# A new order of steps in the first block and in the recurrent block's sixteen slots

## Chip, cores, metric

One core of one Trainium2 chip. The time is device microseconds of one execution, the median of several runs.

## What is computed

Four blocks in a row over `x` (32 x 128 tokens x 512) with the context `ctx` of the same shape, all in float32. Cut to what matters here:

```python
# block 0: attention on the context, 32 query heads and 8 key heads of 16, a mask that is added, then layer norm
q, k, v = x @ Wq + bq, ctx @ Wk + bk, ctx @ Wv + bv
out = softmax(q k^T / 4 + mask) v
x = layernorm(out @ Wo + bo + x) * gamma + beta
# block 1: non-local block, channels are the 128 tokens of a row
g, theta, phi = Wg x + bg, Wtheta x + btheta, Wphi ctx + bphi
x = batchnorm(Wz (softmax(phi^T theta) g) + bz) + x
# block 2: recurrent block, state of 16 x 16 per head, 32 heads
xa = ln(x);  five mixes xk, xw, xv, xr, xg of xa and its shifted rows, by a small LoRA (maa_w1, maa_w2)
w = exp(-exp(time_decay + tanh(xw @ td_w1) @ td_w2));  r, k, v, g = xr Wr, xk Wk, xv Wv, silu(xg Wg)
for t: out_t = r_t (u * k_t v_t + s);  s = k_t v_t + w_t * s
x1 = x + (groupnorm(out) * g) @ Wo
x = x1 + sigmoid(xr2 @ Wfr) * (relu(xk2 @ Wfk)^2 @ Wfv)      # xk2, xr2: mixes of ln(x1) and its shifted rows
# block 3: attention on the context, 16 heads, then an MLP of 2048
```

## The kernel before

Three phases follow each other with a barrier between them: `phase_a` (blocks 0 and 1 but for the batch norm), `phase_b` (the recurrent block, and, in the turns at its two ends, the keys and values of the last block) and `phase_c` (the last block). The change touches two tables, one in `phase_a` and one in `phase_b`; `phase_c` stays.

**How a phase is ordered.** Each phase runs turns. A turn works on a pair of batch rows (16 pairs), and a table written by hand gives the order of its steps with an offset: `("cT", 1)` is the step `cT` of the next pair, `("o1", -1)` that of the pair before. All five engines walk the same table. For each step an engine does its own part: TensorE the matmuls, ScalarE, VectorE and GpSimd what follows, SyncE the transfers in an order of its own. So the table's order is the order in every engine's queue, and a step that waits holds up all that is behind it on that engine. Engines wait for each other only on semaphores, many of them of the form "the n-th result of this kind".

**The ring.** TensorE's results go to four PSUM banks that are used in turn (`Ring`, L81). The items (one per filled bank) are numbered in the table's order; item n may be filled once the item n - 4 is drained, by ScalarE or by VectorE (`ready`, L95). The scores have the other four banks (`pS`) for themselves. A new order of steps is thus a new order of banks, too. A step whose name ends in x only starts the item that its y ends; the item has the place of y.

**phase_a, by step.** `sc0` to `sc3`: scores of half the heads of one row of the pair (TensorE, L423); VectorE adds the mask (L638) and finds the maximum (L642), GpSimd subtracts it (L708). `ta`, `tb`: the transposes of the result in two halves (L432), ScalarE takes the exponential of them (L556). `pv`: probabilities times values, and their sum (L447); VectorE inverts and multiplies (L658, L660). `cT`, `xT`: transposes of context and input (L467). `k`, `v`, `q0`, `q1`: projections. `o0`, `o1`: output projection (L492), VectorE adds the residual and takes the statistics. `xb`: GpSimd adds the bias to the residual. `n0`, `n1`: the layer norm, on VectorE (L675) and GpSimd. `th0`, `th1`: theta, g and phi of block 1. `f0`, `f1`: its scores, into `pS` (L516); maximum on VectorE (L684), exponential on ScalarE (`a_f`, L593). `fr`: VectorE inverts the sums. `fs`: ScalarE scales (L598). `fTa`, `fTb`: transposes (L524). `y`, `wy`: the two last products. `sc0` and `sc2` must wait until the exponentials of `f1` and `f0` have left `pS`; `f0` and `f1` wait until the scores of the same banks are masked. SyncE loads the next pair when `xT` and `cT` are transposed, then the mask, and spreads `kT` over `kexp` in 32 transfers; it stores `x1` when `n0` and `n1` are done.

**phase_b, by step.** Sixteen slots; in front of each slot stands one piece of the scan over time, for the two rows g = 0 and 1: six score products with h = 2 to 64 (`scan`, TensorE L1306), `PRODUCT` (L1314, L1319) and `TURNED` (L1323). After each score product VectorE (h = 2, 4, 8, L1651) or ScalarE (h = 16, 32, 64, L1475) copies the scores into `A`, and GpSimd multiplies the decays into `R` (L1804) and `kT` (L1809). TensorE may start the next score product only when both are done. The steps of the slots have four offsets: `p` (next pair: norm, mixes, w, k, r), `l` (this pair: v, g, the sums `u`, `ut`, `own`), `f` (pair before: group norm, output, second norm, `fk`, `fr`), `e` (two pairs before: `fv`). Those that matter here:
- `stats`, `whiten`, `n1`, `shift`, `h`, `a0`, `a1`: the first norm. Statistics on VectorE (L1541 to L1547), the root on GpSimd (`deviation`, L1748), `(x - mean) * rstd` on VectorE (L1552), transposes (L1211), affine part on ScalarE (L1384), shifted rows and first mix on VectorE (L1559, L1565), then the LoRA (`h` L1229 and L1234, `a0` and `a1` L1245, ScalarE's L1401 and L1403 between them).
- the same under `f` on `x2`: `stats`, `whiten`, `n2`, `shift`, then `fk0`, `fk1` (L1189) and `fr0`, `fr1` (L1202).
- `gn_mean`, `gn_var`, `gn_div`, `gate`: the group norm, on VectorE, with a square (L1489) and a root (L1492, which needs a table load) on ScalarE, and transposes of the result.
- `sum3`, `sum2`, `m4`: GpSimd adds `xT` to the mixes (L1762), which `r`, `v` and `g` need.
- `v`: ScalarE drains it and issues a transfer itself (L1434, L1437); `ut`: ScalarE copies `usum` (L1454).
- `own0`, `own1`, `uk`: VectorE only (L1630 to L1641). `first`: ScalarE splits `rT`, GpSimd starts the next scan.
- `g0x` to `g1y` (L1189): ScalarE's tanh (L1443, which needs a table load), then VectorE's product (L1616).

SyncE's order in the loop of `phase_b` is its own (`turn`): store, read back, save, load.

Of the kernel before, what the change touches and what calls it, by code (L numbers as in the profile page):

```python
# [140 lines left out]
def phase_a(nc, dram, stats, kept):  # L141
# [9 lines left out]


    SLOTS = [
# [5 lines left out]
    ]  # L159
    OFF = {s: off for slot in SLOTS for s, off in slot}  # L160
    ITEMS = {}
# [14 lines left out]
    with ExitStack() as ctx:  # L176
        def sb(name, shape, dt=F32):
            return ctx.enter_context(nc.sbuf_tensor("a_" + name, shape, dt))
# [18 lines left out]
        xT, cT, kT = sb("xT", [P, KC, TOK]), sb("cT", [P, KC, TOK]), sb("kT", [P, TOK])  # L197
# [529 lines left out]
def phase_b(nc, dram, norm, kept):  # L727
# [18 lines left out]

    LAG = {"p": 1, "l": 0, "f": -1, "e": -2}
    SLOTS_OF = [
        [("e", "fv0"), ("p", "x2"), ("l", "v0x")],
        [("e", "fv1"), ("p", "stats")],  # L750
        [("l", "u"), ("l", "v0y"), ("l", "ut")],
        [("p", "whiten"), ("f", "gn_mean"), ("p", "n1"), ("l", "v1"), ("l", "g0x"), ("f", "gn_var"), ("p", "shift")],
        [("f", "gn_div"), ("l", "g0y"), ("l", "g1x"), ("l", "g1y"), ("f", "gate")],
        [("p", "h"), ("l", "own0"), ("p", "a0")],
        [],
        [("p", "a1")],
        [("f", "o0"), ("f", "o1")],
        [("p", "td"), ("p", "sum3"), ("p", "k0x"), ("f", "stats")],
        [("p", "sum2"), ("p", "w"), ("p", "k0y"), ("p", "k1x")],
        [("f", "whiten"), ("p", "k1y"), ("f", "n2")],  # L760
        [("p", "m4"), ("p", "r0"), ("l", "own1")],
        [("f", "shift"), ("p", "r1"), ("p", "first")],
        [("p", "uk"), ("f", "fk0")],
        [("f", "fk1"), ("f", "fr0"), ("f", "fr1")],
    ]

    def fills(kind, step):
# [49 lines left out]
    with ExitStack() as ctx:  # L817
        def sb(name, shape, dt=F32):
            return ctx.enter_context(nc.sbuf_tensor("b_" + name, shape, dt))

        def sig(name, per):
            return Signal(ctx.enter_context(nc.semaphore("b_" + name)), per)
# [17 lines left out]
        x1g, wyg, x2 = kept["x1g"], kept["wyg"], sb("x2", [P, G, D])  # L840
        xn = [sb("xn0", [P, G, D]), sb("xn1", [P, G, D])]
        xT = [sb("xT0", [P, KC, G, T + 1]), sb("xT1", [P, KC, G, T + 1])]
# [49 lines left out]
        gn_centred, gn_squared, gn_var, gn_root, gn_ready = (sig("gn" + n, 1) for n in ("c", "s", "v", "r", "o"))  # L892
# [1392 lines left out]
def program(nc, dram):  # L2285
    with ExitStack() as ctx:
        stats = ctx.enter_context(nc.sbuf_tensor("stats", [P, B * 6], F32))
        norm = ctx.enter_context(nc.sbuf_tensor("norm", [P, 2], F32))
        for n, shape in (("cT", (NG * 2, P, KC, TOK // 2)), ("k", (NG, P, KC, TOK)), ("v", (B, T, D))):
            dram[n] = nc.dram_tensor("mid_" + n, shape, F32, kind="Internal").ap()  # L2290
        def tiles(names, shape):
            return {n: ctx.enter_context(nc.sbuf_tensor("s_" + n, shape, F32)) for n in names}

        kept = {**tiles(("Wfk", "Wfr", "Wfv"), [P, KC, D]), **tiles(("x1g", "wyg"), [P, 2, D])}
        held_before = nc.snapshot_sems()
        phase_a(nc, dram, stats, kept)
        spent = nc.allocated_since(held_before)
        kept.update({**tiles(("Wk", "Wr", "Wv", "Wg"), [P, KC, D]), **tiles(("ident",), [P, P]), **tiles(("vec",), [P, dram["vecs"].shape[1]])})
        phase_norm(nc, dram, stats, norm, spent)
        phase_b(nc, dram, norm, kept)  # L2300
        phase_c(nc, dram, kept)
# [47 lines left out]
```

## Time and profile before

| | us |
|---|---|
| median of 3 runs | 4158.98 (4158.30 to 4162.31) |
| the profiled execution | 4167.61 |
| its span | 4165.8 |
| TensorE busy in it | 3964.3 |
| mean granted clock of TensorE | 0.982 |
| phase_a, to the batch norm's first instruction | 1026.3 |
| a middle turn of phase_a (`sc0` at 324.33 to `sc0` at 383.03) | 58.70 |
| a middle turn of phase_b | 93.75 to 95.20 |

The page gives each engine's busy time as a share of the span. A row of the timeline gives the start in us from the span's start, the duration, the engine, the line of the kernel, the operation, out<-in with shapes, and how many instructions are merged; in brackets how long the engine was idle before it and who released it. Instructions that are merged overlap a little at their ends, so the start of the next row says better than the duration when TensorE was free. `PE` is TensorE, `DVE` VectorE, `ACT` ScalarE, `POOL` GpSimd. The granted clock is a share of 2.4 GHz.

### The profile page before, as it was taken

How to read it: one execution, taken by the hardware profiler on the slowest of the kernel's cores; microseconds unless marked ns; L12 is line 12 of the kernel's file. 1: busy time of each engine (PE TensorE's matmuls, PEld its weight loads, DVE VectorE, ACT ScalarE, POOL GpSimd, SP SyncE). 2: the span in 40 equal slices, each digit the busy share in tenths (PEclk: the TensorE clock that was granted, in tenths of full speed). 3: DMA queues.
4: the chain of work that ended last, by engine and by line, in shares of the span. 5: the costliest groups of instructions: out<-in, count | busy, mean ns of one | idle time of the engine just before them, and what ended most of it. 6: DMA issues, size and time to landing. Idle time of an engine off the chain costs nothing. (4 is left out here: it accounts for less than half of the span.)

```text
span 4165.8 us, 75480 instructions
## 1 busy us (share of the span) xinstructions
PE 3964.3 (95%) x30176; PEld 2490.4 (60%) x30176; DVE 2253.5 (54%) x2705; ACT 1493.8 (36%) x2616; POOL 1407.9 (34%) x1178
## 2 busy tenths in 40 slices
PE   6999999996999999999999999978999999999998
PEld 5666666763666666666666666644544545545543
DVE  3666666663367777767777774325443443434420
ACT  2555555554144344444444433212222322212220
POOL 2333334331255555555555553102121121211210
PEclk8999999998999999999999999989999999999999
DMA  3221222212320010000110002132011010110100
GB/s 103 77 85 64 81 72 80 73 55 80 135 80 31 31 42 31 31 31 33 41 38 31 31 31 90 66 125 91 1 42 42 1 41 7 36 42 1 42 11 10
DMA packets 123614, 211.78 MB, mean 51 GB/s; under 512 B 19296, under 2 KB 39776, under 8 KB 121760
## 3 DMA queue, kind: packets, MB, share of 16 engines
q1 hardware_dynamic: 120736, 200.80, 14.1%
q8 instruction: 254, 4.16, 0.4%
q10 hardware_dynamic: 2560, 6.29, 0.4%
q14 instruction: 64, 0.52, 0.0%
HBM read 125.24 MB, written 67.11 MB: 46 GB/s over the span
## 5 line engine op out<-in xcount | busy, mean ns | idle before, releaser
L2103 PE MATMUL c_pR<-c_proj_w,c_fcT 128*128 128x512 f32 x1024 | 460.2, 598 | 7.2 <-PEq L1953 3.2
L2043 PE MATMUL c_pR<-s_Wfr,c_fc_w 128*128 128x512 f32 x1024 | 456.1, 596 | 4.9 <-ACTq L1953 1.9
L1651 DVE COPY_PREDICATED b_A<-b_mask,b_pS 128x2048 f32<-128x2048 uint32 x96 | 304.4, 3171 | 184.4 <-PE b_pS L1306 183.4
L708 POOL TENSOR_TENSOR a_S<-a_S,a_negmax 128x2048 f32<-128x2048 f32 x64 | 231.0, 3609 | 475.5 <-DVE a_negmax L642 475.5
L1804 POOL TENSOR_TENSOR b_R<-b_R,b_Wh 128x512 f32<-128x512 f32 x192 | 219.1, 1141 | 503.5 <-PE b_pS L1306 503.5
L2043 PEld LDWEIGHTS c_pR<-s_Wfr,c_fc_w 128*128 128x128 f32 x1024 | 192.0, 190 | 241.5 <-issue 238.1
L2103 PEld LDWEIGHTS c_pR<-c_proj_w,c_fcT 128*128 128x128 f32 x1024 | 189.5, 190 | 234.9 <-issue 223.7
L2214 DVE TENSOR_TENSOR c_res<-c_res,c_pR 128x512 f32<-128x512 f32 x128 | 88.0, 687 | 407.4 <-PE c_pR L2103 382.6
L2240 POOL TENSOR_TENSOR c_S<-c_S,c_negmax 128x1024 f32<-128x1024 f32 x64 | 121.3, 1896 | 528.5 <-DVE c_negmax L2186 528.5
L1306 PE MATMUL b_pS<-b_R,b_kT 32*128 32x128 f32 x6144 | 227.4, 284 | 41.9 <-POOL b_kT L1809 27.6
L1306 PEld LDWEIGHTS b_pS<-b_R,b_kT 32*128 32x128 f32 x6144 | 190.5, 187 | 126.7 <-issue 76.5
L2113 ACT ACTIVATE c_fcT<-c_pR,s_vec 128x512 f32<-128x512 f32 x128 | 88.1, 688 | 452.8 <-PE c_pR L2043 423.6
L1762 POOL TENSOR_TENSOR b_xm<-b_xm,b_xT 128x512 f32<-128x512 f32 x160 | 195.2, 1242 | 95.6 <-DVE b_xm L1607 72.8
L638 DVE SCALAR_TENSOR_TENSOR a_S<-a_pS,a_mask 128x2048 f32<-128x2048 f32 x64 | 146.2, 2284 | 132.7 <-PE a_pS L423 132.7
L1475 ACT ACTIVATE b_A<-b_pS 16x512 f32<-16x512 f32 (+2 forms) x224 | 199.6, 891 | 50.6 <-PE b_pS L1306 49.0
L556 ACT ACTIVATE a_probsT<-a_pR 128x512 f32<-128x512 f32 x256 | 138.2, 602 | 190.5 <-PE a_pR L432 190.2
L2194 DVE RECIPROCAL c_rec<-c_pR 128x256 f32<-128x256 f32 x64 | 112.5, 1757 | 161.1 <-PE c_pR L2088 155.0
L658 DVE RECIPROCAL a_rec<-a_pR 128x256 f32<-128x256 f32 x64 | 112.5, 1758 | 116.0 <-PE a_pR L447 111.1
L2225 POOL TENSOR_TENSOR c_rstd<-c_veps,c_half 128x1 f32<-128x1 f32 x64 | 43.3, 676 | 379.9 <-DVE c_veps L2153 379.9
L432 PEld LDWEIGHTS a_pR<-a_ident,a_S 128*128 128x128 f32 x1024 | 115.4, 143 | 58.9 <-issue 58.5
L2113 ACT ACT_TABLE_LOAD x71 | 91.1, 1283 | 161.8 <-PE c_pR L2043 161.1
L642 DVE TENSOR_REDUCE a_negmax<-a_S 128x16 f32<-128x2048 f32 x64 | 146.3, 2286 | 2.2
(262 smaller groups left out, 7879.2 us busy)
## 6 DMA issues: line engine op xcount, KB each, us to landing
a_c<-ctx SPq DMA_DIRECT2D x16, 512.0 KB, 3.6
a_x<-x SPq DMA_DIRECT2D x16, 512.0 KB, 4.6
a_kexp<-a_kT SPq DMA_DIRECT2D x512, 16.0 KB, 1.8
mid_cT<-a_cT SPq DMA_DIRECT2D x16, 512.0 KB, 3.0
a_xl<-x SPq DMA_DIRECT2D x32, 256.0 KB, 3.1
a_cl<-ctx SPq DMA_DIRECT2D x32, 256.0 KB, 3.7
mid_x<-a_xl SPq DMA_DIRECT2D x32, 256.0 KB, 2.5
mid_wy<-a_wy SPq DMA_DIRECT2D x32, 256.0 KB, 2.1
```

The lines of the kernel that those rows point to most:

```text
L556: nc.scalar.activation(probsT[n % 2][:, at:at + 4, :], bank.rearrange("p (h t) -> p h t", h=4), ACT.Exp).then_inc(*emptied["act"].up())
L638: nc.vector.scalar_tensor_tensor(out=S[n % 2][:, :, :], in0=pS[:, :, :].rearrange("p r (h t) -> p (r h) t", t=T), scalar=float(HD) ** -0.5 ...
L642: nc.vector.tensor_reduce(negmax[n % 2][:, :], S[n % 2][:, :, :], AX.X, ALU.max, negate=True).then_inc(*max_found.up())
L708: nc.gpsimd.tensor_tensor(S[n % 2][:, :, :], S[n % 2][:, :, :], negmax[n % 2][:, :].unsqueeze(2).to_broadcast([P, RH, T]), ALU.add)\
L1306: mm = nc.tensor.matmul(pS[:, r, c * P:c * P + P].rearrange("p (e n h) -> p e n h", e=2, h=h), kT[par][at, c, g * T:g * T + T], later, sta ...
L1475: ins = nc.scalar.activation(A[rows, :, 2 * h * b + h:2 * h * b + 2 * h], pS[rows, :, :].rearrange("p r (q t) -> p (r q) t", t=T // 2)[:, ...
L1651: nc.vector.copy_predicated(A[:, :, :].rearrange("p q (n two h) -> p q n two h", two=2, h=h)[:, :, :, 1, :], masks[h][:, :].bitcast(U32).r ...
L1762: nc.gpsimd.tensor_tensor(part, part, xT[0][:, 2 * h:2 * h + 2, :, 1:T + 1].rearrange("p k g t -> p (k g) t"), ALU.add)\
L1804: nc.gpsimd.tensor_tensor(later, later, decay, ALU.mult).then_inc(*r_moved.up())
L2043: mm = nc.tensor.matmul(bank, w[:, c, at * P:at * P + P], src[:, c, :], start=(c == 0), stop=(c == KC - 1))
L2103: mm = nc.tensor.matmul(bank, fcT[part % 2][:, m, g * T:g * T + T], proj_w[:, KC * part + m, :], start=(m == 0), stop=(m == KC - 1))
L2113: nc.scalar.activation(dst, bank, func, **kw).then_inc(*emptied["act"].up())
```

## The change

It gives the steps of the two tables another order. No step is added or removed, no tile changes, and every step keeps its offset. In `phase_a`: `xT` goes in front of `fs1`, `pv3` and `th0`; `xb1` between `fTa1` and `fTb1`; `y1` before `ta0`; `pv0` before `n1`, and `v` behind both and `fr0`; `ta1` from the third slot to the second, before `wy1`; `xb0`, `o0` and `ta2` before `sc3`; `n0` behind `pv2`. In `phase_b` the table of the sixteen slots changes in 13 of them.

```diff
--- before.py
+++ after.py
@@ -151,11 +151,10 @@
 
 
     SLOTS = [
-        [("sc0", 0), ("ta3", -1), ("cT", 1), ("tb3", -1), ("k", 1), ("fs1", -2), ("pv3", -1), ("th0", -1), ("xT", 1), ("fTa1", -2), ("fTb1", -2),
-         ("xb1", -1)],
-        [("sc1", 0), ("o1", -1), ("ta0", 0), ("y1", -2), ("tb0", 0), ("f0", -1), ("v", 1), ("n1", -1), ("pv0", 0), ("fr0", -1), ("wy1", -2)],
-        [("sc2", 0), ("ta1", 0), ("tb1", 0), ("q0", 1), ("fs0", -1), ("pv1", 0), ("th1", -1), ("fTa0", -1), ("fTb0", -1), ("xb0", 0)],
-        [("sc3", 0), ("o0", 0), ("ta2", 0), ("y0", -1), ("tb2", 0), ("f1", -1), ("q1", 1), ("n0", 0), ("pv2", 0), ("fr1", -1), ("wy0", -1)],
+        [("sc0", 0), ("ta3", -1), ("cT", 1), ("tb3", -1), ("k", 1), ("xT", 1), ("fs1", -2), ("pv3", -1), ("th0", -1), ("fTa1", -2), ("xb1", -1), ("fTb1", -2)],
+        [("sc1", 0), ("o1", -1), ("y1", -2), ("ta0", 0), ("tb0", 0), ("f0", -1), ("pv0", 0), ("n1", -1), ("fr0", -1), ("v", 1), ("ta1", 0), ("wy1", -2)],
+        [("sc2", 0), ("tb1", 0), ("q0", 1), ("fs0", -1), ("pv1", 0), ("th1", -1), ("fTa0", -1), ("fTb0", -1)],
+        [("xb0", 0), ("o0", 0), ("ta2", 0), ("sc3", 0), ("y0", -1), ("tb2", 0), ("f1", -1), ("q1", 1), ("pv2", 0), ("n0", 0), ("fr1", -1), ("wy0", -1)],
     ]
     OFF = {s: off for slot in SLOTS for s, off in slot}
     ITEMS = {}
@@ -746,22 +745,22 @@
 
     LAG = {"p": 1, "l": 0, "f": -1, "e": -2}
     SLOTS_OF = [
-        [("e", "fv0"), ("p", "x2"), ("l", "v0x")],
-        [("e", "fv1"), ("p", "stats")],
-        [("l", "u"), ("l", "v0y"), ("l", "ut")],
-        [("p", "whiten"), ("f", "gn_mean"), ("p", "n1"), ("l", "v1"), ("l", "g0x"), ("f", "gn_var"), ("p", "shift")],
-        [("f", "gn_div"), ("l", "g0y"), ("l", "g1x"), ("l", "g1y"), ("f", "gate")],
-        [("p", "h"), ("l", "own0"), ("p", "a0")],
+        [("p", "x2"), ("e", "fv0"), ("l", "v0x")],
+        [("e", "fv1")],
+        [("l", "u"), ("p", "stats"), ("l", "v0y"), ("l", "ut")],
+        [("l", "g0x"), ("f", "gn_mean"), ("p", "whiten"), ("l", "v1"), ("f", "gn_var"), ("p", "n1")],
+        [("f", "gn_div"), ("p", "shift"), ("l", "g0y"), ("l", "g1x"), ("l", "g1y"), ("l", "own0"), ("f", "gate")],
+        [("p", "h"), ("p", "a0")],
         [],
         [("p", "a1")],
         [("f", "o0"), ("f", "o1")],
-        [("p", "td"), ("p", "sum3"), ("p", "k0x"), ("f", "stats")],
-        [("p", "sum2"), ("p", "w"), ("p", "k0y"), ("p", "k1x")],
-        [("f", "whiten"), ("p", "k1y"), ("f", "n2")],
-        [("p", "m4"), ("p", "r0"), ("l", "own1")],
-        [("f", "shift"), ("p", "r1"), ("p", "first")],
-        [("p", "uk"), ("f", "fk0")],
-        [("f", "fk1"), ("f", "fr0"), ("f", "fr1")],
+        [("p", "td"), ("p", "k0x"), ("f", "stats")],
+        [("f", "whiten"), ("p", "w"), ("p", "k0y"), ("p", "sum3")],
+        [("f", "n2"), ("p", "sum2"), ("p", "k1x"), ("p", "k1y"), ("f", "shift")],
+        [("p", "m4"), ("p", "r0")],
+        [("f", "fk0"), ("p", "r1"), ("p", "first"), ("l", "own1")],
+        [("f", "fr0"), ("p", "uk")],
+        [("f", "fk1"), ("f", "fr1")],
     ]
 
     def fills(kind, step):
```

## Rows read from the trace of the kernel before

**Rows 1.** page part 1, busy time by engine over the whole span
```profile
PE 3964.3 (95%) x30176; PEld 2490.4 (60%) x30176; DVE 2253.5 (54%) x2705; ACT 1493.8 (36%) x2616; POOL 1407.9 (34%) x1178
```

**Rows 2.** windows of two turns of the recurrent block: us, busy per engine, clock, DMA
```profile
1702.00:1797.20 95.20, 91.29 (x874) 64.48 (x874) 67.87 (x88) 40.13 (x70) 49.58 (x52) 0.98 0.10 34
2034.93:2128.68 93.75, 89.83 (x875) 63.29 (x874) 68.00 (x87) 40.03 (x71) 49.88 (x51) 1.00 0.10 34
```

**Rows 3.** waits of TensorE: us in total, times, longest
```profile
PE b_pS L1306 <- POOL b_kT L1809: 27.6, 16, 1.9
PE a_pS L423 <- ACT a_f L593: 7.4, 15, 2.3
```

**Rows 4.** timeline, first block: DVE and PE of a middle turn, PE first and last
```profile
367.33 2.29 DVE L638 SCALAR_TENSOR_TENSOR a_S<-a_pS,a_mask 128x2048 f32<-128x2048 f32 x1 [3.08 <-PE a_pS L423]
...
371.63 1.94 PE L532 MATMUL a_pR<-a_fT,a_gx 128*64 128x512 f32 x8
...
84.18 1.06 PE L432 MATMUL a_pR<-a_ident,a_S 128*128 128x128 f32 x8 [1.32 <-DVE a_xl L665]
...
939.81 3.36 PE L432 MATMUL a_pR<-a_ident,a_S 128*128 128x128 f32 x16
```

**Rows 5.** timeline, TensorE, first half of a turn: start, us, line, idle before
```profile
1876.08 1.19 PE L1306 MATMUL b_pS<-b_R,b_kT 32*128 32x128 f32 x32
1890.99 0.38 PE L1292 MATMUL b_pR<-s_ident,b_hid 128*128 128x128 f32 x2
1893.22 1.17 PE L1306 MATMUL b_pS<-b_R,b_kT 32*128 32x128 f32 x32 [1.84 <-POOL b_kT L1809]
1909.15 1.99 PE L1229 MATMUL b_pR<-b_xn,b_w 128*128 128x256 f32 x8
1912.51 1.15 PE L1245 MATMUL b_pR<-b_hid,b_w2a 32*128 32x256 f32 x16 [0.37 <-ACT b_hid L1403]
```

**Rows 6.** timeline, VectorE and GpSimd, the same turn
```profile
1888.72 1.28 DVE L1541 BATCH_NORM_STATS2 b_bn<-s_wyg 128x6 f32<-128x512 f32 x2
1890.64 2.35 DVE L1651 COPY_PREDICATED b_A<-b_mask,b_pS 128x2048 f32<-128x2048 uint32 x1
...
1892.40 0.64 POOL L1809 TENSOR_TENSOR b_kT<-b_kT,b_Wh 128x256 f32<-128x256 f32 x1
```

**Rows 7.** timeline, ScalarE, the same turn
```profile
1892.55 0.39 ACT L1454 ACTIVATE b_usum<-b_pR 128x64 f32<-128x64 f32 x2 [0.67 <-ACT b_v_pad L1434]
1898.11 1.93 ACT L1384 ACTIVATE b_xT<-b_pR,s_vec 128x256 f32<-128x256 f32 x4
1899.92 0.61 ACT L1434 ACTIVATE b_v_pad<-b_pR 128x512 f32<-128x512 f32 x1
1901.06 1.28 ACT L1492 ACT_TABLE_LOAD   x1 [0.53 <-ACT b_v_pad L1434]
```

**Rows 8.** windows of 6 us from the long wait, TensorE alone
```profile
1797.90:1803.90 6.00, 5.93 (x46) 0.72 0.56 199
1893.20:1899.20 6.00, 5.98 (x51) 1.00 0.56 199
```

**Rows 9.** timeline, TensorE, second half of a turn
```profile
1743.40 1.17 PE L1306 MATMUL b_pS<-b_R,b_kT 32*128 32x128 f32 x32
1744.50 1.16 PE L1277 MATMUL b_pR<-s_x1g,b_td 64*128 64x128 f32 x16
1749.25 1.17 PE L1306 MATMUL b_pS<-b_R,b_kT 32*128 32x128 f32 x32
1752.18 1.04 PE L1211 MATMUL b_pR<-s_ident,b_xn 128*128 128x128 f32 x8
```

**Rows 10.** timeline, VectorE and GpSimd, beside it; source L1552
```profile
1747.20 2.88 DVE L1552 TENSOR_SCALAR b_xn<-b_x,b_mv,b_rstd 128x512 f32<-128x512 f32 x2
...
1747.29 2.51 POOL L1762 TENSOR_TENSOR b_xm<-b_xm,b_xT 128x512 f32<-128x512 f32 x2
...
L1552 DVE TENSOR_SCALAR b_xn<-b_x,b_mv,b_rstd x32: 520/1406/1562, 1272.4 to 2760.9; 128x512 f32<-128x512 f32 x32
```

## The prediction

> **What bounds the kernel now.** I read first the page's busy times: TensorE is busy for 3964.3 of 4165.8 us [rows 1], so a new order can win only out of the 201 us in which it is idle, and the last block, which the change leaves alone, holds its share of them. Then windows of one turn each. A turn of the recurrent block takes 93.75 us at full clock and keeps TensorE busy for 89.83; another takes 95.20 with the clock granted at 0.98 [rows 2]. So 3.9 us per turn are waits and 1.45 us are clock. Then TensorE's waits: the largest one that repeats is for GpSimd's `b_kT`, 27.6 us in 16 times, 1.84 in nearly every turn; the first block has one, for ScalarE's exponentials `a_f`, 7.4 us in 15 times [rows 3]. In its middle turns (58.7 us from one `sc0` to the next) the first block has nothing else to win. About 0.2% (8 us) is what a measurement of this kernel can tell from no change. The sum is made against the profiled execution, 4167.61 us (span 4165.8, and 1.8 around it), which lies 8.6 above the median of 4158.98; I carry the difference over to the median.
>
> **First block.** Nothing is added or removed: 48 ring items per turn before and after, each with its own matmuls, drains and transfers. The wait of `sc2` for the exponentials of `f0` goes, because `ta1` (0.97 us of transposes) now stands in front of it; of 7.4 us, 0.29 in each middle turn, I let 0.8 stay in the last turn, where the wait was longest: -6.6. In the first turn `o0` now precedes `sc3` on TensorE and VectorE, so the bank that `tb2` waited 1.32 us for [rows 4] is empty in time: -1.3. The transposes behind the long wait of the last turn took 3.36 us for 16 matmuls, where eight take 1.06: that half clock goes with the wait, -1.3. With `v` behind `pv0`, nothing covers ScalarE's exponentials of `tb0` in the first turn, as `v` did: an estimate of about one pair of them, +0.9. Sum -8, between -10 and 0.
> The rest of this block I cost at nothing, with these covers. `sc3` moves to 2.9 us before `f1`, which overwrites the same PSUM: VectorE's masking takes 2.29 [rows 4], `y0` (1.94, next one 1.87 later) and `tb2` (1.0) cover it by some 0.5 us; if VectorE starts `sc3` 0.6 us late (behind `o0`), `f1` waits. `wy1` comes only 0.3 us after `pv0`'s bank is empty. `xT` moves up by 4.6 us past `pv3` and `th0`: SyncE's queue stands behind it with the loads of the next pair, the mask and 32 copies to `kexp`, which all start that much sooner. The store of `x1` is ahead of these in SyncE's queue and now waits for `n0`, which VectorE does behind `pv2`; that is done before `xT`'s own wait ends, so nothing behind it is held. `th0` needs the same `n0`, which is ready some 4 us before it. GpSimd has `xb0` sooner, in idle time. If both thin covers fail, each costs up to 0.5 us in 14 turns: +14, a part of the range.
>
> **Recurrent block, first half of a turn.** I count from the first scores (1876.08). The fourth scores start at 17.14, though TensorE ended the work before them at 15.3 [rows 5]. What is late is GpSimd's `b_kT`, at 17.0, for it stands in its queue behind the root of `stats`, and VectorE does `stats` (1.28 and 0.6 more) ahead of the copy of 2.35 [rows 6]. The change puts `stats` behind the third scores: the copy then runs from 12.6 to 15.0, GpSimd moves at once, and the wait of 1.84 goes.
> What is late next: `g0x` now follows these scores at once and needs the bank of `ut`, which ScalarE empties at 16.9 (1892.55 and 0.39 [rows 7]); TensorE is there at 16.4: +0.5. From the fourth scores to `h` is 15.93 us of work without a gap (17.14 to 33.07), so `h` could start at 31.7 and `a0` (3.36 later) at 35.1. But `h` needs `shift`, which the change puts behind `gn_div`, and `gn_div` needs ScalarE's root, whose table load stands behind the drain of `v1`. `v1` ends at 22.2 (15.3, 0.5, and 1.1, 1.8 and 3.4 of scores, `g0x` and `v1`). Drain 0.61 and DMA issue 0.47 put the table load at 23.4. Before, it was 11.45 us from the table load (1901.06) to `a0` (1912.51) on a ScalarE with 0.6 us of gaps, and now the four drains of `n1` (1.93, and 0.2 for the first column) lie between too [rows 5, 7]: 23.4 + 11.45 - 0.6 + 2.1 = 36.3; I take 36.2. Before it was 36.43. So of 1.84 us, 0.25 is left: 15 turns give -3.8. Bounds: if these chains don't hold, 1.3 per turn, -20; if they take 1 us longer, +11. `own0`, `fk0` and `first` move within VectorE's, ScalarE's and GpSimd's queues; TensorE's own order puts 3 us or more of work between each and whoever waits for it, and SyncE's loads wait for steps that keep their place: 0.
> The clock: 6 us from the long wait, it was 0.72 of 2.4 GHz in 7 of 15 turns (a part of the stretch at 1.2) and 1.00 in 8, and it fell nowhere else in a middle turn [rows 8]. With the wait, 7 times 1.45 go: -10.2.
>
> **Recurrent block, second half.** From the ninth scores to the turn's end TensorE had no wait at all, so here the change can only lose. `n2`, the transposes of the whitened rows, moves from behind `k1y` to right behind the twelfth scores. TensorE's place then: 1743.40, scores 1.10, `w` 1.10, half of the `k` work 1.85, so the twelfth scores start at 1747.45 (before 1749.25) and `n2` could start at 1748.55 (before 1752.18) [rows 9]. VectorE's whitening starts at 1747.20, right behind a copy in both orders, and takes 2.88 us: to 1750.08. It is slow since GpSimd adds at that moment (1747.29, 2.51 us); the median of one of these two instructions is 1.41, the shortest 0.52 [rows 10]. GpSimd still adds just then, `sum3` in the place of `sum2`. So `n2` waits 1.55 us, in the 14 turns in which it has no units of the last block beside it: +21.7. Bounds: with the shortest whitening (1.04) it ends at 1748.2 and nothing waits, 0; with two of the longest (1.56) 1.8 us, +25.
> A wait of 1.55 can drop the clock as 1.84 did. I take 4 of 14 turns (it is shorter, and full matmuls of `k` stand ahead of it): +5.8, between 0 and +20.
> The Trainium skill (SBUF — State Buffer, Who interferes with whom) says that VectorE and GpSimd share a port pair and that whoever issues first keeps it for the whole instruction, the other blocked. By that rule the place of the adds alone does not say how long the whitening is, only who comes first does, and the trace agrees in that the same instruction takes 0.52 to 1.56 us. It gives a rival below.
>
> **Sum.** -8.3 - 3.8 - 10.2 + 21.7 + 5.8 = +5.2: 4172.8 in a profiled execution like this one, 4164 on the median. Its own range, with half a microsecond per turn for the thin covers and chains, is 4156 to 4172.
>
> **Rivals.**
> (a) VectorE gets in first, the whitening takes 1.04 us, and `n2` waits for nothing: 4164 - 21.7 - 5.8 = 4136. For it: it was 0.52 in some turns, and VectorE starts 0.09 ahead of GpSimd's add. Against: it did so before too and lost in nearly every turn. 0.2.
> (b) The chain over the root is shorter than I add it up, `a0` starts when TensorE is free, and 1 us more per turn is won: 4164 - 16 = 4148. For it: ScalarE's gaps in the rows; against: eleven of its instructions in a row. 0.15.
> (c) Slower: ScalarE becomes the bound of the first half. The table load, `n1`'s drains, the copies to `A`, the tanh load and the gates now stand in one row behind `v1`; once `a0` starts later than 36.4, each turn loses. At 37.3, 1.1 us more per turn: 4164 + 16 = 4180. 0.17.
> (d) The clock falls in every turn behind the new wait: 10 times 1.45 more, 4178. For it: half of the old waits did it; against: eight did not. 0.13.
> My own case: 0.35.
>
> **Numbers.** (a) and (b) are faster, 0.35, less 0.03 for a (b) that wins only half as much and stays within 0.2% (above 4150.7). (c) and (d) are slower, 0.30, and of my own case's 0.35 the part above 4167.3, 0.08. That leaves 0.30 for no change: faster 0.32, same 0.30, slower 0.38. The range 4136 to 4181 takes in (a) to (d) at their prices; what it leaves out, two of them at once on one side or a thin cover of the first block that fails in full, I put at under 0.2.
>
> **What would show it.** Right: no wait of the scores for `b_kT`; a new wait of about 1.5 us of `n2` (L1211) for VectorE's L1552, 14 times; `g0x` (L1189) waiting 0.5 for ScalarE's `b_usum`; waits before `h` and `a0` of about 1 us together for VectorE and ScalarE; a turn of 95 us; the first block 58.4 per turn. Wrong: `n2` without a wait (a), a turn of 92 to 94 us; a wait of 2 us or more at `a0` (c); clock below 1 in each turn (d); or a wait of `f1` or `wy1` in the first block.

## The result and the profile after

The changed kernel takes 4142.70 us (median, 4140.32 to 4144.20) against 4162.31 of the kernel before beside it on the same chip: a ratio of 0.9949, 95% interval 0.9937 to 0.9960. The profiled execution takes 4144.2 us with a span of 4142.5, 23.3 below the span before. It is faster by 0.5%, where I had forecast no change with a lean to slower.

The page's busy times of the changed kernel:

```profile
PE 3944.2 (95%) x30176; PEld 2480.6 (60%) x30176; DVE 2246.4 (54%) x2705; ACT 1487.9 (36%) x2616; POOL 1412.2 (34%) x1178
```

By the medians it is 19.6 us less. TensorE does the same 30176 matmuls in 20.1 us less busy time [rows 1], and its idle time falls by only 3.2. So most of the net gain is not in waits, where new ones nearly make up for those that went: it is in a higher clock and in shorter groups of matmuls.

Windows of the changed kernel: one middle turn of the first block, then one of the recurrent block (columns as in rows 2).

```profile
520.35:578.34 57.99, 57.96 (x568) 40.12 (x564) 38.22 (x37) 31.74 (x65) 23.04 (x12) 1.00 0.23 76
```

```profile
2043.97:2137.95 93.98, 89.66 (x875) 63.37 (x874) 67.27 (x87) 39.83 (x70) 50.01 (x50) 1.00 0.10 34
```

The same turn of the first block, in the kernel before:

```profile
524.00:582.70 58.70, 58.38 (x567) 40.23 (x565) 37.97 (x36) 31.88 (x65) 23.04 (x12) 1.00 0.22 75
```

The first matmul of the recurrent block starts at 1019.04 instead of 1032.50, so the first block gives 13.5 us. From there to the last block's first matmul it is 1765.5 us instead of 1775.1, so the recurrent block gives 9.6. A recurrent turn without a dip took 93.75 us [rows 2] and takes 93.97 now: the new order itself loses 0.2 us per turn. What it wins is that no turn from the third on takes 95.2 any more, and seven did. The second turn still has a lower clock and is even longer, here in the kernel before and then in the changed one:

```profile
1211.32:1306.29 94.97, 91.53 (x876) 63.96 (x876) 65.34 (x85) 37.98 (x67) 53.57 (x57) 0.98 0.22 78
```

```profile
1196.56:1292.16 95.60, 92.30 (x875) 64.95 (x875) 64.45 (x85) 37.66 (x67) 53.66 (x57) 0.97 0.22 78
```

TensorE's waits in the changed kernel:

```profile
PE b_pR L1210 <- DVE b_xn L1551: 17.7, 14, 1.4
PE b_pR L1244 <- ACT b_hid L1402: 9.5, 16, 0.7
PE b_pR L1188 <- ACT b_usum L1453: 7.6, 16, 0.5
```

The wait for `b_kT` [rows 3] is down to 1.4 us in all, in one place. `n2` now waits for the whitening 14 times: 1.41 to 1.43 us in the 12 middle turns, and 0.3 in the first and in the last of the 14. The timeline shows the new waits in one turn, TensorE first, then VectorE and GpSimd beside `n2`, then ScalarE:

```profile
2043.97 1.19 PE L1305 MATMUL b_pS<-b_R,b_kT 32*128 32x128 f32 x32
...
2060.89 1.99 PE L1188 MATMUL b_pR<-b_xm,s_Wg 128*128 128x256 f32 x8 [0.50 <-ACT b_usum L1453]
...
2079.32 1.15 PE L1244 MATMUL b_pR<-b_hid,b_w2a 32*128 32x256 f32 x16 [0.55 <-ACT b_hid L1402]
...
2105.90 1.09 PE L1210 MATMUL b_pR<-s_ident,b_xn 128*128 128x128 f32 x8 [1.43 <-DVE b_xn L1551]
```

```profile
2102.97 2.88 DVE L1551 TENSOR_SCALAR b_xn<-b_x,b_mv,b_rstd 128x512 f32<-128x512 f32 x2
...
2103.06 2.51 POOL L1761 TENSOR_TENSOR b_xm<-b_xm,b_xT 128x512 f32<-128x512 f32 x2
```

```profile
2066.35 0.60 ACT L1433 ACTIVATE b_v_pad<-b_pR 128x512 f32<-128x512 f32 x1 [1.53 <-PE b_pR L1201]
...
2067.48 1.28 ACT L1491 ACT_TABLE_LOAD   x1 [0.53 <-ACT b_v_pad L1433]
```

Counted from the first scores (2043.97), `a0` starts at 35.35, where the forecast had 36.2 and the kernel before 36.43 [rows 5].

### The profile page after: what moved, and what is told of

It is laid out like the page before. It is cut to its first block and busy times, and to the rows that moved or that the text cites. A ratio compares the mean times of both kernels' runs of the same rounds, so it can differ in the third digit from the quotient of the medians.

```text
span 4142.5 us, 75479 instructions
## 1 busy us (share of the span) xinstructions
PE 3944.2 (95%) x30176; PEld 2480.6 (60%) x30176; DVE 2246.4 (54%) x2705; ACT 1487.9 (36%) x2616; POOL 1412.2 (34%) x1178
## 5 line engine op out<-in xcount | busy, mean ns | idle before, releaser
L1803 POOL TENSOR_TENSOR b_R<-b_R,b_Wh 128x512 f32<-128x512 f32 x192 | 229.7, 1197 | 436.2 <-PE b_pS L1305 436.0
L1305 PEld LDWEIGHTS b_pS<-b_R,b_kT 32*128 32x128 f32 x6144 | 190.2, 186 | 99.2 <-issue 74.4
L1305 PE MATMUL b_pS<-b_R,b_kT 32*128 32x128 f32 x6144 | 226.8, 283 | 15.1 <-POOL b_R L1803 9.7
```

The lines of the kernel that those rows point to most:

```text
L1305: mm = nc.tensor.matmul(pS[:, r, c * P:c * P + P].rearrange("p (e n h) -> p e n h", e=2, h=h), kT[par][at, c, g * T:g * T + T], later, sta ...
L1803: nc.gpsimd.tensor_tensor(later, later, decay, ALU.mult).then_inc(*r_moved.up())
```

## The experiments

All eleven were compared with the kernel before on the same chip. It took 4164.5 us beside the first eight and 4163.5 beside the last three. Line numbers are those of the kernel before or, where the new list of the first block is in, one less (L1305 for L1306).

### Each block alone

```
first run:  SLOTS as in the changed kernel, SLOTS_OF as before
second run: SLOTS as before, SLOTS_OF as in the changed kernel
```

> Only the new order of the first block; the recurrent block keeps its old one. Theory (the two traces add up by block): 13.5 us less than the kernel before, a middle turn of the first block of 58.0 us instead of 58.7, its 0.3 us wait of sc2 gone, and the recurrent block as before: waits for b_kT of 27.6 us and turns of 95.2 next to turns of 93.8. Rival (only the removed waits count, as the prediction had it, and the rest of the difference between the two traces was the chip's): 8 us less and a middle turn of 58.4.

Measured: 4147.8 us, ratio 0.9961 (0.9947 to 0.9975); the recurrent block starts at 1015.8 instead of 1032.5, and the turns and the waits for `b_kT` (27.6 us) are the old ones, with five turns of 95.15 to 95.33. The first block's 13.5 us are real; 8 us is too little. How large it is to a microsecond can't be said from one execution: in the profiled executions of six kernels with this table the recurrent block starts at 1015.8 to 1022.1, and in those of four kernels with the old one at 1029.0 to 1032.6. The middle turns are the same to 0.01 us in all of them; what differs is the turns at the start.

> Only the new order of the recurrent block. Theory: 9.6 us less than the kernel before, turns of 93.97 us throughout, no turn with a clock below 1.00, n2 waiting 1.4 us in 14 turns. Rival (the clock's dips depend on what ran before the block, not on the order in a turn): turns of 95.4 us appear again in about half of the turns, and the time is that of the kernel before or above it.

Measured: 4157.96 us, ratio 0.9982 (0.9973 to 0.9991), 6.5 us less, on 11 runs. No turn behind the second is above 94.1 us (the second takes 94.3, at a clock of 0.98). So the dips of the middle turns go with the order in the turn, not with what ran before the block. The two parts add up: 3.9 and 1.8 thousandths against 5.1.

This run held a surprise. `n2` waited 1.42 us in nine turns, but 0.3 to 0.4 in five. VectorE and GpSimd in a turn of the one kind, then of the other:

```profile
1644.00 1.85 DVE L1552 TENSOR_SCALAR b_xn<-b_x,b_mv,b_rstd 128x512 f32<-128x512 f32 x2
...
1736.97 2.87 DVE L1552 TENSOR_SCALAR b_xn<-b_x,b_mv,b_rstd 128x512 f32<-128x512 f32 x2
```

```profile
1644.09 2.80 POOL L1762 TENSOR_TENSOR b_xm<-b_xm,b_xT 128x512 f32<-128x512 f32 x2
...
1737.06 2.49 POOL L1762 TENSOR_TENSOR b_xm<-b_xm,b_xT 128x512 f32<-128x512 f32 x2
```

In both turns VectorE starts 0.09 us ahead of GpSimd. In one the whitening takes 1.85 us and the additions 2.80, in the other 2.87 and 2.49. It is a race that is decided anew in each turn, for 1.0 us. The short form came in 3 of the 12 middle turns here. The other two of the five are the first and the last of the 14, where VectorE starts 0.17 to 0.19 us ahead; these two are short in the kernel before and in the changed one, too. This is rival (a) of the prediction, but at 1.85 us and not at 1.04.

### The second half undone, and n2 alone

```
slots 0 to 5 of SLOTS_OF as in the changed kernel, slots 9 to 15 as before; SLOTS as in the changed kernel
```

> The changed kernel with slots 9 to 15 of the recurrent block back in their old order; slots 0 to 5 stay new. Theory (the two halves are independent, the second one only loses): the wait of n2 goes, a turn takes 92.7 us, and the time is 19 us below the changed kernel, 42 below the kernel before. Rival (what n2 waits for is only moved: with the second half undone, something else of the half waits, or the first half loses its gain because fr0, fr1 and fv come later): a turn of 93.5 us or more, and at most 7 us below the changed kernel.

```diff
-        [("f", "n2"), ("p", "sum2"), ("p", "k1x"), ("p", "k1y"), ("f", "shift")],
+        [("p", "sum2"), ("p", "k1x"), ("p", "k1y"), ("f", "n2"), ("f", "shift")],
```

> The changed kernel with one step moved: n2 behind k1y again, where the kernel before has it (shift stays behind it). Theory: the wait of 1.42 us is the price of n2's place alone; it goes in 14 turns, 17.7 us and a little more for what follows it, so 18 to 20 us below the changed kernel, turns of 92.6. Rival (the second half is bound by what n2 feeds: its four drains, shift and fk0 are late by the same amount, and fk0 or fr0 waits instead): less than 8 us gained, and a new wait behind n2 in the profile.

Measured: 4127.86 us, ratio 0.9914 (0.9901 to 0.9928), turns of 92.64; and 4127.10 us, ratio 0.9908 (0.9893 to 0.9923), turns of 92.73. Both are 15 us below the changed kernel by the medians, 17.0 and 14.7 by the spans. One step in one place is the whole cost of the second half, and everything else in it costs nothing (the two turns differ by 0.1 us). The expected 18 to 20 was a little too much: a turn wins 1.24 of the 1.42 us that `n2` waited.

### What slows the whitening

```diff
-        [("f", "whiten"), ("p", "w"), ("p", "k0y"), ("p", "sum3")],
-        [("f", "n2"), ("p", "sum2"), ("p", "k1x"), ("p", "k1y"), ("f", "shift")],
+        [("f", "whiten"), ("p", "w"), ("p", "k0y")],
+        [("f", "n2"), ("p", "sum3"), ("p", "sum2"), ("p", "k1x"), ("p", "k1y"), ("f", "shift")],
```

> The changed kernel with sum3 (GpSimd's two additions, no work of TensorE) behind n2 instead of beside the whitening. Theory (the whitening is slow because GpSimd adds at the same moment): the two instructions take 1.04 us together instead of 2.88, the wait of n2 falls from 1.42 to about 0 us, a turn takes 92.6 us, and the time is 18 us below the changed kernel, as in the run with n2 moved back. Rival (the whitening is slow whatever GpSimd does, or another GpSimd instruction meets it): n2 waits 1.0 us or more, and the time is within 5 us of the changed kernel's.

Measured: 4132.72 us, ratio 0.9926 (0.9912 to 0.9939). The whitening's source line in the changed kernel, then in this one (ns: shortest, median, longest):

```profile
L1551 DVE TENSOR_SCALAR b_xn<-b_x,b_mv,b_rstd x32: 514/1399/1566, 1258.2 to 2737.9; 128x512 f32<-128x512 f32 x32
```

```profile
L1551 DVE TENSOR_SCALAR b_xn<-b_x,b_mv,b_rstd x32: 509/536/567, 1260.8 to 2729.9; 128x512 f32<-128x512 f32 x32
```

With GpSimd's additions elsewhere the same instruction falls from 1399 to 536 ns, and `n2` waits no more. The cause is the two engines' meeting, as the theory had it. By the Trainium skill (SBUF — State Buffer, Who interferes with whom) this `tensor_scalar` is a kind that can take the shared port pair, and issue order decides who blocks. The trace agrees that the two slow each other when they meet. It doesn't show the second part: in the two kinds of turn above VectorE starts first by the same 0.09 us, and the outcome differs. The turn came to 93.05 us, though, not 92.6: GpSimd is now late by its additions at the product of the scores:

```profile
PE b_pS L1313 <- issue: 2.7, 8, 0.4
PE b_pS L1313 <- POOL b_R L1824: 1.8, 6, 0.3
```

That is 0.3 us in each of 14 turns, so a quarter of a turn's gain went into a wait that neither theory had. Moving `n2` is the cheaper cure.

### Why the first half needs all its moves

```diff
-        [("e", "fv1"), ("p", "stats")],
-        [("l", "u"), ("l", "v0y"), ("l", "ut")],
+        [("e", "fv1")],
+        [("l", "u"), ("p", "stats"), ("l", "v0y"), ("l", "ut")],
```

> The kernel before with one step moved: stats of the recurrent block from slot 1 to behind u in slot 2. Theory (the order of n1 had to move with stats): the scores no longer wait 1.84 us for b_kT, but the whitening that n1 needs now starts some 2 us later, n1 stands right behind these scores and waits about 2.4 us for VectorE's b_xn; the time is that of the kernel before, or up to 9 us above it, and the clock's dips stay. Rival (the wait of 1.84 us is simply gone): turns of 92.0 us without dips and 38 us less.

Measured: 4209.89 us, ratio 1.0110 (1.0095 to 1.0126): 45 us slower, five times the most that I expected. TensorE's `n1` and VectorE's whitening in one turn:

```profile
1916.94 1.92 PE L1211 MATMUL b_pR<-s_ident,b_xn 128*128 128x128 f32 x8 [3.29 <-DVE b_xn L1552]
```

```profile
1914.83 2.05 DVE L1552 TENSOR_SCALAR b_xn<-s_wyg,b_mv,b_rstd 128x512 f32<-128x512 f32 x2 [0.81 <-POOL b_rstd L1748]
```

The wait moved to where the theory put it, but it is 3.3 us: I had left out the 0.8 in which VectorE waits for GpSimd's root, and again reckoned too little for a whitening that meets GpSimd (2.05 us, where it took 0.97 in the kernel before). And with a wait of this length the clock fell in every one of the 15 turns: the eight transposes take 1.92 to 1.97 us instead of 1.04, and turns take 96.7 and 97.8.

The next run moves `n1` as well:

```diff
-        [("p", "whiten"), ("f", "gn_mean"), ("p", "n1"), ("l", "v1"), ("l", "g0x"), ("f", "gn_var"), ("p", "shift")],
+        [("p", "whiten"), ("f", "gn_mean"), ("l", "v1"), ("l", "g0x"), ("p", "n1"), ("f", "gn_var"), ("p", "shift")],
```

> The run with only stats moved, and n1 moved with it, behind g0x; shift and gn_mean keep their old places, and n1 stands ahead of gn_var. Theory (what the wait for b_kT gave back is decided by where the table load for the root of gn_var stands on ScalarE; here it is behind n1's drains, at 24.9 us from the first scores, as before): the waits for b_kT and of n1 are gone, the time comes back as longer waits at the transposes of o, at h or at a0, a turn of 93.2 to 93.8 us without dips of the clock, 8 to 18 us below the kernel before. Rival (the rest of the half has slack, any order without the wait of 1.84 us wins it in full): a turn of 92.0 us and 35 us less.

Measured: 4204.82 us, ratio 1.010 (1.008 to 1.0119), 41 us slower. Neither theory had a loss. ScalarE, VectorE and TensorE:

```profile
1916.74 1.28 ACT L1492 ACT_TABLE_LOAD   x1
```

```profile
1919.61 0.55 DVE L1675 RECIPROCAL b_grstd<-b_grstd 128x64 f32<-128x64 f32 x1
...
1921.19 1.22 DVE L1685 TENSOR_TENSOR b_o<-b_o,b_grstd 128x1024 f32<-128x1024 f32 x1
```

```profile
1922.55 1.97 PE L1211 MATMUL b_pR<-s_ident,b_o 128*128 128x128 f32 x8 [3.29 <-DVE b_o L1685]
```

The load for the root stands at 26.6 us from the first scores (1890.13) and not at 24.9, behind `n1`'s drains, and VectorE does `shift` (1.22 and 1.67 us) ahead of the division that begins with the reciprocal above, so the transposes of `o` wait 3.29. The place was named right (the transposes of `o`), its size wrong, and behind it the clock dips in every middle turn again. What the change does that neither of these runs does is to put `gn_var` ahead of `n1` and `shift` behind `gn_div`; in it neither wait appears. Which of the two moves counts for more was not run.

### What holds a0

On the kernel with `n2` back:

```diff
-        [("l", "g0x"), ("f", "gn_mean"), ("p", "whiten"), ("l", "v1"), ("f", "gn_var"), ("p", "n1")],
+        [("f", "gn_mean"), ("l", "v1"), ("p", "whiten"), ("l", "g0x"), ("f", "gn_var"), ("p", "n1")],
```

> The kernel with n2 back behind k1y, and v1 ahead of g0x in slot 3 of the recurrent block, right behind gn_mean. Theory (a0 stands behind an unbroken row of ScalarE that begins with the drain of v1 and the table load for the root): v1 takes over the wait of 0.5 us for b_usum, its drain is done 1.1 us earlier, the table load starts 1.1 us earlier, and the waits before h and a0 (0.2 and 0.55 us) go; a turn of 92.0 us and 4116 in all, 11 below the run with n2 back. Rival (the row of VectorE from gn_mean on or the whitening sets h and a0): the waits stay, a turn of 92.6 to 92.7, the time as with n2 back.

Measured: 4114.86 us, ratio 0.9885 (0.987 to 0.990), the fastest kernel of this study, 1.15% below the one before and 12 us below the run with `n2` back. Its turn, its table load and its `a0` (first scores at 2024.06):

```profile
2024.06:2115.91 91.85, 89.77 (x875) 63.37 (x874) 67.65 (x87) 39.58 (x70) 51.83 (x50) 1.00 0.10 35
```

```profile
2046.26 1.28 ACT L1491 ACT_TABLE_LOAD   x1 [0.53 <-ACT b_v_pad L1433]
```

```profile
2058.66 1.15 PE L1244 MATMUL b_pR<-b_hid,b_w2a 32*128 32x256 f32 x16 [0.37 <-ACT b_hid L1402]
```

The load starts at 22.2 instead of 23.5, `a0` at 34.6 instead of 35.35, and `h` waits no more. The 0.37 us left at `a0` is the trip of its own input from TensorE over ScalarE, as in the kernel before [rows 5]. So in the changed kernel ScalarE's row behind `v1` did hold `a0`. One thing came better than expected: `v1` does not take over the wait of 0.5 us; it starts at 2040.61, right behind the scores.

### Where the first block's 0.71 us per turn comes from

`v` ahead of `pv0`, on the changed kernel:

```diff
-        [("sc1", 0), ("o1", -1), ("y1", -2), ("ta0", 0), ("tb0", 0), ("f0", -1), ("pv0", 0), ("n1", -1), ("fr0", -1), ("v", 1), ("ta1", 0), ("wy1", -2)],
+        [("sc1", 0), ("o1", -1), ("y1", -2), ("ta0", 0), ("tb0", 0), ("f0", -1), ("v", 1), ("n1", -1), ("pv0", 0), ("fr0", -1), ("ta1", 0), ("wy1", -2)],
```

`ta1` ahead of `wy1`, on the kernel before:

```diff
-        [("sc1", 0), ("o1", -1), ("ta0", 0), ("y1", -2), ("tb0", 0), ("f0", -1), ("v", 1), ("n1", -1), ("pv0", 0), ("fr0", -1), ("wy1", -2)],
-        [("sc2", 0), ("ta1", 0), ("tb1", 0), ("q0", 1), ("fs0", -1), ("pv1", 0), ("th1", -1), ("fTa0", -1), ("fTb0", -1), ("xb0", 0)],
+        [("sc1", 0), ("o1", -1), ("ta0", 0), ("y1", -2), ("tb0", 0), ("f0", -1), ("v", 1), ("n1", -1), ("pv0", 0), ("fr0", -1), ("ta1", 0), ("wy1", -2)],
+        [("sc2", 0), ("tb1", 0), ("q0", 1), ("fs0", -1), ("pv1", 0), ("th1", -1), ("fTa0", -1), ("fTb0", -1), ("xb0", 0)],
```

`sc3` behind `ta2`, on the kernel before:

```diff
-        [("sc3", 0), ("o0", 0), ("ta2", 0), ("y0", -1), ("tb2", 0), ("f1", -1), ("q1", 1), ("n0", 0), ("pv2", 0), ("fr1", -1), ("wy0", -1)],
+        [("o0", 0), ("ta2", 0), ("sc3", 0), ("y0", -1), ("tb2", 0), ("f1", -1), ("q1", 1), ("n0", 0), ("pv2", 0), ("fr1", -1), ("wy0", -1)],
```

> The changed kernel with v ahead of pv0 again in slot 1 of the first block; no wait is expected anywhere. Theory (a group of full 128x128 matmuls costs some 0.1 us more when its neighbour uses a part of the array, so an order with one more such border costs more): v takes 1.98 us from start to start instead of 1.89, a middle turn takes 58.1 to 58.2 us instead of 58.0, and the time is 1 to 3 us above the changed kernel's, too little for the times and to be read in the turn. Rival (the durations do not depend on neighbours; the 0.4 us of the turn were waits that the trace does not show): a middle turn of 58.0 us.

> The kernel before with ta1 of the first block ahead of wy1, and nothing else. Theory (wait and borders between full and partial groups both count): the wait of 0.29 us goes, and the four groups around it take 0.12 us less, a middle turn of 58.3 us instead of 58.70, and 5 to 6 us less in all. Rival (only the wait counts): 58.41 and 4 us less, or 58.5, if ta1 and tb1 apart cost more than together.

> The kernel before with sc3 of the first block behind o0 and ta2, next to y0, and nothing else; it has no wait there before. Theory (two groups that use a part of the array stand side by side, and two borders with full groups go): a middle turn of 58.5 us instead of 58.70, no new wait of f1, 2 to 3 us less in all. Rival (the thin cover of f1 is too thin: f1 waits for VectorE's mask by 0.1 to 0.5 us per turn, or neighbours cost nothing): 58.7 us or more.

Measured: 4146.63 us (ratio 0.9956, 0.9942 to 0.9970), 4158.13 (0.9984, 0.9974 to 0.9994) and 4161.80 (0.9991, 0.9982 to 1.0001). The last can't be told from no change by its times, and the first can't be told from the changed kernel. In the traces the middle turns of one kernel agree to 0.01 us. One of each, in the same order:

```profile
518.56:576.66 58.10, 58.07 (x567) 40.13 (x565) 38.17 (x36) 31.72 (x65) 23.06 (x12) 1.00 0.23 76
```

```profile
524.68:582.97 58.29, 58.26 (x566) 40.15 (x564) 38.09 (x36) 31.90 (x65) 23.09 (x12) 1.00 0.23 76
```

```profile
527.69:586.19 58.50, 58.18 (x566) 40.16 (x564) 38.16 (x36) 31.88 (x65) 23.05 (x12) 1.00 0.23 76
```

`v` behind `pv0` is worth 0.11 us, `ta1` ahead of `wy1` 0.41 (0.29 of it the wait), `sc3` behind `ta2` 0.20. Together that is 0.72, and the change won 0.71; the moves of `xT`, `xb1`, `y1` and `n0` were not run alone, and nothing is left over for them in a middle turn. The third run shows a price as well that a middle turn does not: its second turn takes 62.3 us, where the kernel before takes 57.3 and the changed one 56.7, with new waits of 2.2 and 1.4 us and a clock of 0.97.

The place of the gain is visible within one trace. In the changed kernel the same 16 transposes `fT` stand once ahead of scores, which use a row group of 32, and once ahead of `o`, which uses the full array:

```profile
506.24 1.91 PE L523 MATMUL a_pR<-a_ident,a_f 128*128 128x128 f32 x16
508.08 1.15 PE L422 MATMUL a_pS<-a_kexp,a_qT 32*128 32x256 f32 x16
...
534.26 1.91 PE L523 MATMUL a_pR<-a_ident,a_f 128*128 128x128 f32 x16
536.01 3.60 PE L491 MATMUL a_pR<-a_wo,a_attT 128*128 128x512 f32 x8
539.44 1.04 PE L431 MATMUL a_pR<-a_ident,a_S 128*128 128x128 f32 x8
...
567.14 3.70 PE L491 MATMUL a_pR<-a_wo,a_attT 128*128 128x512 f32 x8
570.78 1.94 PE L531 MATMUL a_pR<-a_fT,a_gx 128*64 128x512 f32 x8
```

From start to start the transposes take 1.84 in the one case and 1.75 in the other, with no wait in either. `o0`, between full groups, takes 3.43, and `o1`, between `sc1` and `y1` that both use a part of the array, 3.64. The Trainium skill (TensorEngine Tiling (Array Packing), Key Properties) says that a change of the tiling mode drains the engine; the trace agrees in direction, at some 0.1 us a time; whether these 0.1 us are a drain no run shows. The thin cover of `f1` held: no wait of it in a middle turn of any of these kernels. That of `wy1` failed once, in the last turn of the changed kernel, by 1.3 us.

## Why the prediction was wrong, point by point

**First block.** I forecast -8.3, and it is -13.5. The wait for `a_f` went as forecast: 7.4 us [rows 3] are down to 0.5. What failed is "The rest of this block I cost at nothing, with these covers": I looked for what could go wrong and not at what the groups cost beside new neighbours. That is 0.42 us in each of 13 turns, 5.4 us, which is the whole difference. Three runs price its parts. That the rest fits to 0.2 us is in part luck, since the turns at the start differ by more from one execution to the next.

**The wait for b_kT** went, and `g0x` waited 0.50 us in its place, as forecast.

**The chain over the root** is the step that failed most, by 12.4 of the 28.5 us. My sum, "23.4 + 11.45 - 0.6 + 2.1 = 36.3; I take 36.2", begins right: the table load is at 23.5. From there to `a0` it is 11.84 us, not 12.95. Of the 11.45 before I took off one gap of ScalarE, 0.6 us, where there were two. ScalarE's timeline of the kernel before, in that turn, and of the changed one:

```profile
1905.85 0.60 ACT L1443 ACTIVATE b_gT<-b_pR 128x512 f32<-128x512 f32 x1
1907.09 0.60 ACT L1443 ACTIVATE b_gT<-b_pR 128x512 f32<-128x512 f32 x1 [0.64 <-PE b_pR L1189]
1907.72 1.93 ACT L1499 ACTIVATE b_z<-b_pR,s_vec 128x256 f32<-128x256 f32 x4
...
1911.28 0.38 ACT L1401 ACTIVATE b_hid<-b_pR 128x256 f32<-128x256 f32 x1
1912.19 0.27 ACT L1403 ACTIVATE b_hid<-b_pR 64x128 f32<-64x128 f32 x1 [0.52 <-PE b_pR L1234]
```

```profile
2074.18 1.08 ACT L1442 ACTIVATE b_gT<-b_pR 128x512 f32<-128x512 f32 x2
2075.15 1.94 ACT L1498 ACTIVATE b_z<-b_pR,s_vec 128x256 f32<-128x256 f32 x4
...
2078.71 0.38 ACT L1400 ACTIVATE b_hid<-b_pR 128x256 f32<-128x256 f32 x1
2078.97 0.28 ACT L1402 ACTIVATE b_hid<-b_pR 64x128 f32<-64x128 f32 x1
```

The two gaps are 0.64 and 0.52, but from start to start they cost more, since without a gap an instruction begins before the last has ended: from `gT` to `z` it is 1.87 us before and 0.97 now, and from the first `hid` to the second 0.91 and 0.26. Together that is 1.55 us, where I took off 0.6. And I added `n1`'s drains by their durations, 2.1, where they add 1.9 from start to start. With both the sum is 11.45 - 1.55 + 1.9 = 11.8, as measured. The first half wins 1.08 us per turn instead of 0.25, 16 us instead of 3.8. That is rival (b), 0.83 us more per turn where it named 1, and I gave it 0.15. The chain itself is real: the run with `v1` first shortens it and `a0` follows. Rival (c), the same chain grown longer, was the wrong way round.

**The clock.** "With the wait, 7 times 1.45 go" held: from the third turn on none of 95.2 is left, -10.2. The seven were this execution's: three other kernels with the same wait had 5, 5 and 4. "A wait of 1.55 can drop the clock as 1.84 did", +5.8, did not come, and with it rival (d) falls: in the three kernels with this wait it was 1.35 to 1.43 us long 32 times, and none of these turns was above 94.2 us.

**The second half.** Forecast +21.7; a turn loses 1.34 us there, +18.8. Place, cause and count were right, but the wait was 1.43 instead of 1.55, and only 0.3 in two of the 14. Rival (a) had its own price wrong. The 0.52 us that it drew on was in the kernel before only the first instruction of a pair whose second took 1.4, or a whitening with no addition beside it. So where VectorE gets in first, the pair takes 1.85 us and not 1.04, and `n2` waits 0.3 to 0.4 and not nothing. It came so in none of the 12 middle turns of the changed kernel, in one of the kernel with `v` ahead of `pv0` and in three of the run with this block alone; a range for each turn, not for the kernel, would have said it better. That this one step was the second half's whole price stood too: putting it back gives 15 us.

**The sum.** From +5.2 to -23.3 it is 28.5 us: 12.4 the root chain, 5.8 the new dips, 5.2 the neighbours, 2.9 the size of the wait of `n2`, and 2.2 that these counts of 14 and 15 turns do not place. It lies at the two ends of the recurrent block: its first turn is 1.3 us shorter and its second 0.6 longer, and the last of the fifteen is shorter by 1.2 us beyond its dip. Each error had the same sign: the change was charged too much at every step, and what a new neighbour or an overlap gives back was not looked for.

## What to carry to other kernels

When a row of instructions on one engine is carried from one order to another, subtract every gap in it and add starts, not durations; here an error of 0.8 us per turn was enough to turn the sign of the forecast. Moving a step of statistics was not one move here: its normalised output, the root beside it and the shift behind it moved with it, and the runs with one or two of the four lost 1% where all four win. Then look for the one step of the new order that waits: undoing `n2` and putting `v1` ahead of `g0x` took the gain from 0.5% to 1.15%.

## What the runs showed of the hardware

- **Neighbours.** A group of full-array matmuls costs 0.09 to 0.11 us more for each neighbour that uses part of the rows or columns, with no wait shown; an order with fewer such borders took 0.42 us off a turn of 58.70.
- **The race of two engines.** VectorE's whitening (two instructions) that starts 0.09 us ahead of GpSimd's additions takes 1.85 us in some turns, 2.87 in most, and 0.98 where these additions stand elsewhere.
- **The clock.** The wait of 1.84 us comes in 13 turns. The clock fell behind 7 of them in the kernel before, and behind 5, 5 and 4 in three kernels that kept it. Behind `n2`'s wait of 1.35 to 1.43 us it fell in none of 32. With a wait of 3.3 us it fell in every turn. The length of one wait doesn't settle it, though: the scores that open the second turn wait 1.42 us, shortly behind a wait of 2.00, and there the clock is low, 0.51 over six microseconds in the changed kernel:

```profile
1194.48 0.66 PE L1322 MATMUL b_pS<-s_ident,b_oT 128*128 128x128 f32 x4 [2.00 <-ACT b_oT L1479]
1196.56 2.09 PE L1305 MATMUL b_pS<-b_R,b_kT 32*128 32x128 f32 x32 [1.42 <-POOL b_kT L1808]
```

```profile
1196.56:1202.56 6.00, 6.00 (x37) 0.51 0.00 0
```

The six microseconds behind the long wait with `stats` moved, and those behind `n2`'s wait in the changed kernel:

```profile
1916.90:1922.90 6.00, 5.96 (x16) 0.72 0.18 66
```

```profile
2105.90:2111.90 6.00, 6.00 (x66) 1.00 0.08 25
```

The first has the clock at 0.72, a part of it at 1.2 GHz, the second is at 2.4 throughout. Why a wait of 1.84 drops the clock in some turns and not in others was not tried.
